# Attention in query tiles of 512 tokens instead of 384, in a two-layer conv/attention kernel

## What is computed

```python
f = _l2norm(feats.reshape(B * N, C))
scores = jnp.matmul(f, f.T) / TEMPERATURE
attn = jax.nn.softmax(scores, axis=-1)
feats_att = jnp.matmul(attn, f)
feats_fcm = f * W_BLEND + feats_att * (1.0 - W_BLEND)
return _l2norm(feats_fcm.reshape(B, N, C))
```

## Time and profile before

| what | value |
|---|---|
| median of 3 runs | 6354.89 us (6354.02 to 6360.9) |
| the profiled execution, its own time | 6360.01 us |
| its span, first to last instruction | 6358.2 us |
| PE busy, share of the span | 5222.5 us, 82% |
| PE weight loads busy | 3620.2 us, 57% |
| DVE busy | 4292.1 us, 68% |
| POOL busy | 4214.9 us, 66% |
| ACT busy | 3922.1 us, 62% |
| first score matmul of attention to its last output matmul | 4651.9 to 5571.7 us |

### The profile page before, as it was taken

One profiled execution on the slowest core, in us unless ns is written; L12 is line 12 of the kernel. 1 busy time (PEld: TensorE's weight loads), 2 busy tenths in 40 slices (PEclk: granted clock), 3 DMA queues, 4 the chain that ended last, 5 costly groups with the idle time before them and its releaser, 6 DMA issues. The chain is left out here.

```text
span 6358.2 us, 87285 instructions
## 1 busy us (share of the span) xinstructions
PE 5222.5 (82%) x22860; PEld 3620.2 (57%) x22860; DVE 4292.1 (68%) x4355; ACT 3922.1 (62%) x8591; POOL 4214.9 (66%) x2811
## 2 busy tenths in 40 slices
PE   4766489999898998998989989755599999956994
PEld 2333255555555555555555555422389999935773
DVE  2666589999999999999999999765231111154332
ACT  2555588888888888888888888644522222232332
POOL 0455689999999999999999999732034444402441
PEclk8888699999999999999999999967799999965996
DMA  3354477777777777777777777664200000012213
GB/s 91 138 187 178 186 238 249 251 243 251 238 249 242 246 250 237 248 249 239 251 249 244 250 249 245 230 215 141 74 1 0 0 0 0 0 55 88 84 58 109
DMA packets 399686, 1073.56 MB, mean 169 GB/s; under 512 B 51470, under 2 KB 94511, under 8 KB 393600
## 3 DMA queue, kind: packets, MB, share of 16 engines
q1 hardware_dynamic: 387808, 1043.07, 49.8%
q0 software_dynamic: 7584, 20.72, 1.0%
q10 hardware_dynamic: 3840, 4.72, 0.3%
HBM read 883.39 MB, written 184.94 MB: 168 GB/s over the span
## 5 line engine op out<-in xcount | busy, mean ns | idle before, releaser
L912 POOL TENSOR_TENSOR scan_hc<-scan_h,scan_c_rep 128x768 f32<-128x768 f32 x1536 | 2749.5, 1824 | 228.1 <-PE scan_ps_y L743 176.7
L743 PE MATMUL scan_ps_y<-scan_hc,keep_ident 128*128 128x512 f32 (+1 forms) x6144 | 2219.5, 489 | 23.6 <-ACT scan_y L778 23.2
L877 DVE TENSOR_TENSOR_SCAN scan_h<-scan_da,scan_h,scan_ps_p 128x768 f32<-128x768 f32 x896 | 1568.0, 1795 | 0.0
L743 PEld LDWEIGHTS scan_ps_y<-scan_hc,keep_ident 128*128 128x128 f32 x6144 | 1067.6, 190 | 823.7 <-issue 738.7
L795 ACT ACTIVATE scan_warm<-scan_du_t 128x128 f32<-128x128 f32 x4608 | 1423.8, 388 | 40.4 <-PE scan_ps_p L734 34.7
L834 ACT ACTIVATE scan_da<-scan_dd,layer_a_neg 128x768 f32<-128x768 f32 x1344 | 1184.5, 922 | 5.5 <-issue 2.8
L1254 POOL TENSOR_TENSOR attn_e_lo<-attn_e,attn_e_hi 128x384 fp32r<-128x384 f32 x432 | 437.1, 1012 | 761.8 <-DVE attn_e_hi L1245 761.8
L734 PE MATMUL scan_ps_p<-keep_ident,scan_warm 128*128 128x128 f32 x4608 | 647.4, 277 | 221.9 <-DVE scan_h L877 221.0
L877 DVE TENSOR_TENSOR_SCAN scan_h<-scan_da,scan_ps_p 128x768 f32<-128x768 f32 x448 | 758.4, 1734 | 2.2 <-ACT scan_da L834 2.0
L734 PEld LDWEIGHTS scan_ps_p<-keep_ident,scan_warm 128*128 128x128 f32 x4608 | 532.6, 142 | 372.0 <-issue 162.4
L856 DVE TENSOR_TENSOR scan_ps_p<-scan_ps_p,scan_dd 128x768 f32<-128x768 f32 x576 | 546.8, 949 | 186.2 <-PE scan_ps_p L726 185.0
(11 more groups left out here) (285 smaller groups left out, 7408.4 us busy)
## 6 DMA issues: line engine op xcount, KB each, us to landing
scan_c_rep<-bc_dram SPq DMA_DIRECT2D x1536, 384.0 KB, 4.2
scan_dd<-dd_dram SPq DMA_DIRECT2D x96, 768.0 KB, 5.7
scan_b_rep<-bc_dram SPq DMA_DIRECT2D x192, 384.0 KB, 4.8
dd_dram<-delta_de SPq DMA_DIRECT2D x96, 384.0 KB, 6.0
dd_dram<-delta_du SPq DMA_DIRECT2D x96, 384.0 KB, 7.1
y_dram<-scan_y SPq DMA_DIRECT2D x96, 384.0 KB, 4.5
merge_y<-y_dram SPq DMA_DIRECT2D x32, 1152.0 KB, 10.6
delta_img<-xn_dram SPq DMA_DIRECT2D x16, 576.0 KB, 9.5
```

Source lines behind the costliest of these rows:

```text
L743: mm = pe.matmul(ps_y[:, lo:hi], keep["ident"][:, :], hc[t % HR][:, lo:hi], start=n == 0, stop=n == N - 1)
L877: dve.tensor_tensor_scan(view(h[n]), view(x), view(y), start, ALU.mult, ALU.add).then_inc(scan_done, 1)
L912: pool.tensor_tensor(hc[t % HR][:, :], h[t % N][:, :], c_rep[t % CR][:, :], ALU.mult).then_inc(hc_done, 1)
```

## The change

TT stays 384 for all other phases. Attention gets a tile size of its own, QT = 512, and NQ = 9 tiles. Each score and output matmul, exponential, cast, subtraction and copy of `ps_o` works on 512 columns in place of 384. `e`, `e_hi` and `e_lo` have three copies each instead of four, indexed with j % 3; the four tiles `ps_s` stay, indexed with j % 4. `den` has 9 columns per key block instead of 12. The order of the instructions on every engine is the same; the outer loop runs 9 times instead of 12. Per engine and loop: 5184 matmuls of 384 columns become 3888 of 512 (columns in all: 1,990,656 both times), 432 exponentials, casts and subtractions become 324, 12 copies of `ps_o` become 9.

```diff
--- before.py
+++ after.py
@@ -37,6 +37,8 @@
 TT = 384
 NTT = NT // TT
 TPI = L // TT
+QT = 512
+NQ = NT // QT
 KB = NT // 128
 E, HF = 8, 512
 HB = HF // 128
@@ -1180,9 +1182,9 @@
         s = Space(nc, ctx, "attn")
         t_hi = s.sb("t_hi", [128, KB, C], F32R)
         t_lo = s.sb("t_lo", [128, KB, C], F32R)
-        e = [s.sb(f"e{i}", [128, TT]) for i in range(4)]
-        e_hi = [s.sb(f"e_hi{i}", [128, TT], F32R) for i in range(4)]
-        e_lo = [s.sb(f"e_lo{i}", [128, TT], F32R) for i in range(4)]
+        e = [s.sb(f"e{i}", [128, QT]) for i in range(3)]
+        e_hi = [s.sb(f"e_hi{i}", [128, QT], F32R) for i in range(3)]
+        e_lo = [s.sb(f"e_lo{i}", [128, QT], F32R) for i in range(3)]
         ps_s = [s.ps(f"ps_s{i}", [128, 512]) for i in range(4)]
         ps_o = s.ps("ps_o", [128, 2, 512])
         turned, moved = s.sem("turned"), s.sem("moved")
@@ -1204,13 +1206,13 @@
 
             def scores(q, j):
                 for h in range(2):
-                    keys, tokens = slice(j * 128, j * 128 + 128), bass.ds(q * TT, TT)
-                    mm = products(pe, ps_s[j % 4][:, 0:TT], (f_hi[:, h, keys], f_hi[:, h, tokens]),
+                    keys, tokens = slice(j * 128, j * 128 + 128), bass.ds(q * QT, QT)
+                    mm = products(pe, ps_s[j % 4][:, 0:QT], (f_hi[:, h, keys], f_hi[:, h, tokens]),
                                   (f_lo[:, h, keys], f_lo[:, h, tokens]), h == 0, h == 1)
                 mm.then_inc(s_full, 1)
 
             pe.sem_inc(o_read, 1)
-            with pe.Fori(0, NTT) as q:
+            with pe.Fori(0, NQ) as q:
                 scores(q, 0)
                 scores(q, 1)
                 for j in range(KB):
@@ -1221,16 +1223,16 @@
                     pe.wait_ge(lo_done, q * KB + j + 1)
                     for o in range(2):
                         ch = slice(o * 128, o * 128 + 128)
-                        mm = products(pe, ps_o[:, o, 0:TT], (t_hi[:, j, ch], e_hi[j % 4][:, :]),
-                                      (t_lo[:, j, ch], e_lo[j % 4][:, :]), j == 0, j == KB - 1)
+                        mm = products(pe, ps_o[:, o, 0:QT], (t_hi[:, j, ch], e_hi[j % 3][:, :]),
+                                      (t_lo[:, j, ch], e_lo[j % 3][:, :]), j == 0, j == KB - 1)
                 mm.then_inc(o_full, 1)
 
         @block.scalar
         def _(act):
-            with act.Fori(0, NTT) as q:
+            with act.Fori(0, NQ) as q:
                 for j in range(KB):
                     act.wait_ge(s_full, q * KB + j + 1)
-                    act.activation(e[j % 4][:, :], ps_s[j % 4][:, 0:TT], ACT.Exp,
+                    act.activation(e[j % 3][:, :], ps_s[j % 4][:, 0:QT], ACT.Exp,
                                    accum_out=den[:, j, bass.ds(q, 1)]).then_inc(e_done, 1)
 
         @block.vector
@@ -1239,19 +1241,19 @@
                 dve.wait_ge(turned, n + 1)
                 t, j = (t_hi if n < KB // 2 else t_lo), 2 * (n % (KB // 2))
                 dve.tensor_copy(t[:, j:j + 2, :].rearrange("p a c -> p (a c)"), ps_s[n % 4][:, :]).then_inc(moved, 1)
-            with dve.Fori(0, NTT) as q:
+            with dve.Fori(0, NQ) as q:
                 for j in range(KB):
                     dve.wait_ge(e_done, q * KB + j + 1)
-                    dve.tensor_copy(e_hi[j % 4][:, :], e[j % 4][:, :]).then_inc(hi_done, 1)
+                    dve.tensor_copy(e_hi[j % 3][:, :], e[j % 3][:, :]).then_inc(hi_done, 1)
                 dve.wait_ge(o_full, q + 1)
-                dve.tensor_copy(o_t[:, :, bass.ds(q * TT, TT)], ps_o[:, :, 0:TT]).then_inc(o_read, 1)
+                dve.tensor_copy(o_t[:, :, bass.ds(q * QT, QT)], ps_o[:, :, 0:QT]).then_inc(o_read, 1)
 
         @block.gpsimd
         def _(pool):
-            with pool.Fori(0, NTT) as q:
+            with pool.Fori(0, NQ) as q:
                 for j in range(KB):
                     pool.wait_ge(hi_done, q * KB + j + 1)
-                    pool.tensor_tensor(e_lo[j % 4][:, :], e[j % 4][:, :], e_hi[j % 4][:, :].bitcast(F32), ALU.subtract).then_inc(lo_done, 1)
+                    pool.tensor_tensor(e_lo[j % 3][:, :], e[j % 3][:, :], e_hi[j % 3][:, :].bitcast(F32), ALU.subtract).then_inc(lo_done, 1)
 
 
 def blend_phase(nc, P, keep, f_hi, f_lo, o_t, den):
@@ -1903,7 +1905,7 @@
         o_t = s.sb("o_t", [128, 2, NT])
         with ExitStack() as attn:
             f_hi, f_lo = (attn.enter_context(nc.sbuf_tensor(n, [128, 2, NT], F32R)) for n in ("f_hi", "f_lo"))
-            den = attn.enter_context(nc.sbuf_tensor("den", [128, KB, NTT], F32))
+            den = attn.enter_context(nc.sbuf_tensor("den", [128, KB, NQ], F32))
             project_phase(nc, P, keep, f_hi, f_lo)
             attention_phase(nc, keep, f_hi, f_lo, o_t, den)
             blend_phase(nc, P, keep, f_hi, f_lo, o_t, den)
```

## The result

| | before | after |
|---|---|---|
| median of 7 runs each | 6358.31 us (6352.01 to 6378.05) | 6335.12 us (6322.01 to 6344.77) |
| profiled execution, its own time | 6360.01 us | 6322.01 us |
| its span | 6358.2 us | 6320.1 us |
| attention loop, first score matmul to the end of the last output matmul | 920.1 us | 898.6 us |
| last output matmul's end to the end of the span | 786.1 us | 787.2 us |

The ratio is 0.996, with a 95% interval of 0.9949 to 0.9971: 0.3 to 0.5% faster. The medians differ by 23.2 us; I had forecast 10.8. The loop is 21.5 us shorter in the profile. That part is scatter.

What follows compares the result with a forecast made beforehand. PE was taken to bound the attention loop. Matmuls -4.1, stalls -6.9 and the end of attention +0.2 sum to -10.8 us, from 6354.9 to 6344.1 us, with a range of 6337 to 6351.5.

Steps and rivals of the forecast that it cites:

- PE bounds the loop, 920.1 us, with 24 stalls of 0.42 and a step of 0.1755: Attention loop before the change: PE sets the pace, standing still twice in each of 12 tiles, 10.1 us together.
- Copies cost nothing: Attention buffers: nothing waits for a copy, so three instead of four cost nothing and no wait takes its place.
- The stalls, -6.9 us: PE waits at both ends of query tiles: 24 of 0.42 us become 18 of 0.18, 10.1 to 3.2 us.
- Casts held behind POOL, hidden: Start of a tile: the second cast is held by POOL's subtraction, but o(0) and s(3) cover it; no cost.
- The last copy and the sum over `den`, +0.2: End of attention: the last output copy costs +0.28 us, the shorter sum gives -0.11; together +0.2 us.
- Fewer and longer matmuls, -4.1 us: Attention's matmul stream: 3888 at 0.233 us make 905.9 instead of 910.0 us; bounds -8.0 to -0.2.
- no stalls at all: Rival, attention loop: stalls vanish and the step is at its lower bound; -17.9 us, 6337.0 us; chance 12%.
- My own sign of being wrong: Attention's matmuls: the prediction is wrong if, among other signs, the step leaves 0.230 to 0.237 us.
- no difference that can be told: Whole kernel: the change in time stays too small to tell from none, about 0.2% (12.7 us); chance 0.58.
- that of the weight loads: Rival, attention's matmuls: each costs one weight load whatever its columns, leaving 682 us, 227 less; chance 2%.
- The clock after attention: Rival, blend to gate: the alternating clock falls otherwise, losing at most 35 us; chance 4%.
- A step of 0.239: Rival, attention's matmuls: freshly written data or whole PSUM tiles lengthen the step; kernel 16.6 us slower, 6371.5; chance 2%.

Runs made afterwards that it cites:

- e2: Kernel before (12 tiles of 384) with three copies of e, e_hi and e_lo instead of four; attention loop 920.5 us, step 175.6 ns.
- e1: Changed kernel with four copies of e, e_hi and e_lo instead of three; attention loop 898.7 us, step 230.0 ns.
- e10: Changed kernel with the first expert product taken four times over, 24 matmuls in a row; expert steps 233.3 ns from the tenth on.
- e3: Changed kernel with QT = 256, 18 tiles and three copies; attention loop 941.3 us, step 118.1 ns.
- e4: Changed kernel with 324 DMAs of 192 KB into spare tiles during attention; loop 898.5 us, step 229.9 ns.
- e8: Changed kernel with two transposes into a spare PSUM tile behind each score group; loop 969.4 us, later output-group steps 230.4 ns.
- e12: As e10, but all tiles use expert 0's weights at fixed addresses, without register instructions; expert steps 233.3 ns from the tenth on.
- e9: As e6, but PE waits for the low parts once per pair of output groups; loop 901.3 us, step 229.3 ns away from stalls.
- e13: Changed kernel with its 9 query tiles written out instead of looped over; loop 897.4 us, step 230.0 ns.
- e6: Changed kernel with four copies, two score groups in a row and then two output groups; loop 891.8 us, step 229.3 ns.
- e5: Changed kernel with four copies and scores three key blocks ahead of the outputs instead of two; loop 893.7 us.
- e7: Kernel before (384 columns, four copies) with scores three key blocks ahead instead of two; loop 914.8 us, step 176.4 ns.

## Why the prediction was wrong

Point by point, by its steps.

- *PE bounds the loop, 920.1 us, with 24 stalls of 0.42 and a step of 0.1755*: right, and e2 repeats it.
- *Copies cost nothing*: right, shown at both widths by e1 and e2.
- *The stalls, -6.9 us*: right in its mechanism. The chain grew by 0.51 us as reckoned, the cover by less than reckoned (0.66 us and not 0.69), because the step it is made of is shorter. Measured -5.9. The lower bound of 0.06 us that I gave for one stall does not follow from its own terms: 0.49 + 0.44 - 0.70 late, less 0.12 of slack, is 0.11. The measured 0.23 lies within either.
- *Casts held behind POOL, hidden*: right. They are held for up to 1.02 us, and no wait appears beyond the 18.
- *The last copy and the sum over `den`, +0.2*: +0.16.
- *Fewer and longer matmuls, -4.1 us*: this is the term that failed. It measured -15.6. I priced 3888 matmuls at the 0.233 of rows 5, with 0.232 to 0.234 as bounds; they cost 0.2300, outside the bounds. The 3 ns make 11.5 us; less the 1.0 by which the stalls gave less than forecast, that is the whole of the miss in the loop (21.5 measured, 11.0 forecast).

The rows were read rightly: the expert phase does cost 233 ns, and e10 gives 233.3 even in a run four times as long. What was wrong was to take them for attention's, and to take a straight line through three points from two phases for a confirmation. The 256-column row happens to agree with attention (118.1 in e3), and so the line looked sound while its upper end was not. The bounds came from two readings of the same rows, so they held reading error and nothing of the step from one stream to another. The trace of before had a better start: attention's own steps. With one column a cycle at the granted 2.4 GHz, 128 more columns take 53.3 ns. From the 173.3 ns of the scores in a row at a tile's start that makes 226.6, the lower bound which was missing (881 us of stream). From the 175.5 of the mixed stream it makes 228.8, so 889.6 us, an estimate from the numbers of before together with the column's price, which the three widths later bore out. Measured were 894.3.

One number came near by luck: the rival *no stalls at all* had 6337.0 us, close to the measured 6335.1, but its mechanism is not what happened, since 18 stalls stayed and the step was 2 ns under its 0.232. My own sign of being wrong, a step outside 0.230 to 0.237, was too wide to speak: 0.2300 stands on its edge while the term is 11.5 us off. The likeliest outcome that I named, no difference that can be told (0.58), did not come; the interval, 0.3 to 0.5% faster, does not reach zero. My 6344.1 was counted down from 6354.9, the median of three runs; seven runs give 6358.3, so the forecast time is nearer to the measured one than the forecast difference is.

Of the rivals, that of the weight loads got its answer too. Their share of the window fell from 99 to 81% while PE stayed the bound and the loop got 2.3% shorter. The Trainium skill, "Perfetto Trace Analysis", section "Identifying the Most-Contended Engine", judges TensorE's headroom by the share of peak arithmetic and the share of time in weight loads; by the loads alone, this loop had 1% of it before the change and 19% after. By the rows its limit was columns plus 13.3 ns both times, and the share of loads says little here. The clock after attention did not matter: from the last output matmul to the end it is 786.1 us before and 787.2 after. A step of 0.239 was the wrong way round.

What stays open is why the same instruction costs 227, 230 or 233 ns. Excluded as the cause of 233 in the expert phase: DMA (e4), breaks (e8), a stream too short to settle (e10), registers (e12), and the other engines' work beside it (the window of e10). Excluded as the cause of 230 in the mixed order: copies (e1), the wait (e9), the register instruction (e13). e6 shows that fewer changes between scores and outputs lower it, by 0.5 ns against e5 and 0.7 against the changed kernel, and that the steps behind a change are the long ones. What is left for the expert phase is the tiles themselves, by place or by values. Which expert's weights are read is not it, since e10 with eight experts' and e12 with one's have the same step; the rest was not tried.

## What to carry to other kernels

Take the step of an instruction from the stream that will run it; where a row of another phase must serve, first check it against the own stream at the width that is to be priced, and if that can't be done let the range hold the difference between phases. Agreement at one width is not enough: at 256 columns the two phases agree here, and at 512 they differ by 3 ns. Multiply a small doubt by the count before calling a term small: 3 ns were nearly 12 us here, more than every other term. In a matmul stream with weights of 128 columns, widening from 384 to 512 gave 1.7% of the stream; the rest of the gain was stalls. Grouping scores and outputs by twos with the room for a fourth copy gave another 7 us, of which e5 shows 5 to be had by scores three ahead alone.

## What the runs showed that I had not expected

- A stream of scores that runs undisturbed settles within some eight matmuls at 120.0, 173.3 and 226.7 ns for 256, 384 and 512 columns: one column a cycle and 13.3 ns. Mixed with outputs the steps take a fixed pattern with a period of twelve matmuls, the same in each tile.
- Putting the scores three key blocks ahead took the stalls away at both widths, but at 384 columns it lengthened the step from 175.5 to 176.4 ns (e7), while at 512 it did not (229.8 in e5).
- The phases ahead of attention scatter by nearly 40 us from run to run (their end at 4634 to 4673 us) with code that is the same in all these kernels, while the attention loop repeats within 0.5 us.
